# Cross-attention and mixture-of-experts layer: a second load of the next block's rows for in-place normalisation, and H's fp32 copy kept in PSUM

## The reference

```python
x = x + xattn(layernorm(x), ctx_768, ...)
x = x + ffn(layernorm(x), ...)

def xattn(x, y, ...):
    q = (x @ Wq + bq); k = (y @ Wk + bk); v = (y @ Wv + bv)      # 16 heads of 32
    attn = softmax(einsum('bnhd,bmhd->bhnm', q, k) * scale)
    out = einsum('bhnm,bmhd->bnhd', attn, v).reshape(B, N, 512)
    h = relu(out @ W1 + b1)                                      # 1024 wide
    return h @ W2 + b2

def ffn(x, ...):
    top1 = argmax(x @ Wg.T)
    xhat = (x - mu) * rsqrt(var + 1e-5)
    # each token gets its expert's  gelu((xhat * s_e + b_e) @ w1 + b1) @ w2 + b2
```

## Time and profile before

| | us |
|---|---|
| median of three runs (1581.66 to 1583.35) | 1581.79 |
| the profiled execution | 1584.45 |
| its span, first to last instruction | 1582.6 |
| TensorE matmul busy | 1515.4 (96%) |
| VectorE busy | 1037.9 (66%) |
| ScalarE busy | 713.1 (45%) |
| GpSimd busy | 441.9 (28%) |

### The profile page before, as it was taken

How to read it: one execution, slowest core, us unless ns; L and a number is a source line. 1 busy time by engine, 2 the same in 40 slices (tenths; PEclk the granted TensorE clock), 3 DMA queues, 4 the chain that set the end, 5 groups by cost and what they waited for, 6 DMA issues and landing times.

```text
span 1582.6 us, 24339 instructions
## 1 busy us (share of the span) xinstructions
PE 1515.4 (96%) x7988; PEld 1254.6 (79%) x7988; DVE 1037.9 (66%) x2496; ACT 713.1 (45%) x2015; POOL 441.9 (28%) x312
## 2 busy tenths in 40 slices
PE   6799999999999999999999999999999999997998
PEld 3688788787878787878787788878787878776886
DVE  5756566675758576766666675757575757467776
ACT  2545445353535363635444353535353636333443
POOL 3422122121222222212131122122222222136776
PEclk8899999999999999999999999999999999999999
DMA  9200101112020202020101101010101011548773
GB/s 230 80 28 1 54 1 40 42 31 74 3 86 1 74 14 74 22 75 21 61 27 54 34 23 38 17 54 1 54 1 54 1 54 54 215 153 261 232 226 112
DMA packets 67736, 105.93 MB, mean 67 GB/s; under 512 B 26967, under 2 KB 35432, under 8 KB 66591
## 3 DMA queue, kind: packets, MB, share of 16 engines
q1 hardware_dynamic: 56814, 70.68, 15.9%
q0 software_dynamic: 10800, 33.70, 5.5%
HBM read 59.47 MB, written 46.72 MB: 67 GB/s over the span
## 4 chain that ended last, share of the span: by engine, by line
PE 60%; DVE 23%; DMA 7%; ACT 4%; issue 3%; POOL 2%; DVEq 0%; POOLq 0%; SPq 0%; ACTq 0%
PE bank L1025 13%; PE bank L1050 12%; PE bank L887 11%; PE bank L911 5%; PE bank L1005 5%; DMA region<-rows,pos 4%; DVE actH L994 4%; PE bank L1455 4%; PE bank L1499 4%; DMA rows<-in_x 3%; DVE xn L845 2%; POOL region L1193 2%; ACT actH L988 2%; PE bank L1119 2%; PE bank L1438 2%
## 5 line engine op out<-in xcount | busy, mean ns | idle before, releaser
L1050 PE MATMUL bank<-w,actH 128*128 128x512 f32 x1536 | 373.8, 393 | 4.6 <-DVE actH L1040 4.6
L1025 PE MATMUL bank<-actA,w 128*128 128x512 f32 x1536 | 366.7, 394 | 0.0
L1025 PEld LDWEIGHTS bank<-actA,w 128*128 128x128 f32 x1536 | 286.0, 188 | 62.2
L1050 PEld LDWEIGHTS bank<-w,actH 128*128 128x128 f32 x1536 | 282.4, 188 | 62.9 <-DVE actH L1040 8.6
L970 POOL TENSOR_TENSOR E<-E,rc 128x1232 f32<-128x1232 f32 x64 | 145.0, 2265 | 447.6 <-DVE rc L965 447.6
L1040 DVE TENSOR_TENSOR actH<-htmp,actH 128x512 fp32r<-128x512 f32 x128 | 88.7, 693 | 166.8 <-ACT actH L1036 148.1
L1035 ACT ACTIVATE htmp<-bank,b 128x512 f32<-128x512 f32 x128 | 88.2, 689 | 226.1 <-PE bank L1025 217.4
L887 PE MATMUL bank<-actA,wq 128*128 128x512 f32 x768 | 182.0, 390 | 0.0
L943 ACT ACTIVATE E<-bank,mx 128x77 f32<-128x77 f32 x512 | 157.6, 365 | 45.4 <-DVE mx L920 45.4
L887 PEld LDWEIGHTS bank<-actA,wq 128*128 128x128 f32 x768 | 144.2, 188 | 30.4 <-issue 0.5
L1193 POOL DMA_INDIRECT region<-rows,pos x64 | 63.1, 985 | 373.0 <-DVE pos L1187 333.9
(11 more groups left out here) (165 smaller groups left out, 2063.3 us busy)
## 6 DMA issues: line engine op xcount, KB each, us to landing
rowB<-region SPq DMA_DIRECT2D x71, 258.0 KB
rows<-in_x SPq DMA_DIRECT2D x64, 256.0 KB, 3.5
e_raw<-in_E SPq DMA_DIRECT2D x16, 256.0 KB, 2.7
region<-padrow SPq DMA_DIRECT2D x9, 258.0 KB, 2.6
w_raw<-in_W SPq DMA_DIRECT2D x1, 2048.0 KB, 10.3
w_raw<-in_W SPq DMA_DIRECT2D x2, 1024.0 KB, 8.5
e_parts<-e_high SPq DMA_DIRECT2D x8, 256.0 KB, 2.0
e_parts<-e_low SPq DMA_DIRECT2D x8, 256.0 KB, 2.3
```

What stands on the lines that cost most here:

```text
L1025: mm = pe.matmul(p[:], w, a, start=k == 0 and j == 0, stop=k == KD - 1 and j == 2)
L1050: mm = pe.matmul(p[:], a, w, start=m == 0 and j == 0, stop=m == MF - 1 and j == 2)
```

## The change

Three things change, and some steps move.

The rows of the next block are loaded a second time, into four buffers `xn` of their own (step `XNLOAD`, in two halves, after H chunks 0 and 2). The statistics are taken from these, and all four tiles are normalised in place at the end of the chain. The step XSTAT moves from behind chunk 5, where three pieces were given out at once, to behind chunk 4. The rows proper are still loaded behind the scatter.

The addition of b2 to the rows becomes a step of its own, `XB`, on GpSimd. It waits for the landing of the rows and no longer for xn. In the setup the XLOAD of block 0 goes behind VLOAD, and its XB behind XLOAD(1).

ScalarE writes the fp32 value of an H chunk back into the chunk's PSUM bank, behind the high part, and VectorE's subtraction reads it from there. The bank is handed on after that subtraction. `htmp` is gone; E1 and E2 both use the memory of the four xn, and the steps that load and split E2 stand later.

```diff
-    xn = [sb(f"xn{i}", [P, D]) for i in range(2)]
+    xn = [sb(f"xn{i}", [P, D]) for i in range(SUB)]
-    htmp = [sb(f"htmp{i}", [P, BLK]) for i in range(2)]
...
-        step("XLOAD", 0)
+        step("XNLOAD", 0, 0)
+        step("XNLOAD", 0, 2)
         step("XSTAT", 0)
...
         step("VLOAD", 0)
+        step("XLOAD", 0)
...
         step("XLOAD", 1)
+        for s in range(SUB):
+            step("XB", 0, s)
...
+                if not last and m in (0, 2):
+                    step("XNLOAD", b + 1, m)
...
-                if m == MF - 3 and not last:
+                if m == MF - 4 and not last:
                     step("XSTAT", b + 1)
-                    step("DRIP", 3)
...
                 step("YA", b, 0)
-                if prep is not None:
-                    step("E2_RAW", prep)
+                for s in range(SUB):
+                    step("XB", b + 1, s)
                 step("Y", b, 0)
...
-            "H": lambda b, m: (S["act_hh"], MF * b + m + 1),
+            "H": lambda b, m: (S["dve_h"], MF * b + m + 1),
...
+        def sp_xnload(sp, b, s0):
+            for s in (s0, s0 + 1):
+                if b:
+                    sp.wait_ge(S["pe_xT"], SUB * (b - 1) + s + 1)
+                if PREP0 + 2 <= b < PREP0 + 2 + NE:
+                    sp.wait_ge(st_e1 if s0 else st_e2, 32 * (b - PREP0 - 1))
+                sp.dma_start(xn[s][:], A["x"][b * BLK + P * s:b * BLK + P * s + P, :]).then_inc(ld_xn[s], 16)
...
-                    dve.wait_ge(ld_x[b % 2][s], 16 * (b // 2 + 1))
-                    n = issued(dve.bn_stats(bn[:, s, :], rows[b % 2][:, s, 0:D]))
+                    dve.wait_ge(ld_xn[s], 16 * (b + 1))
+                    n = issued(dve.bn_stats(bn[:, s, :], xn[s][:]))
...
-                for s in range(2):
-                    dve_xn(dve, b, s)
+                for s in range(SUB):
+                    dve.tensor_scalar(xn[s][:], xn[s][:], mvx[:, s, 0:1], rx[:, s:s + 1],
+                                      ALU.subtract, ALU.mult).then_inc(S["dve_xn"], 1)
...
-            if s + 2 < SUB:
-                dve_xn(dve, b, s + 2)
-
-        def pool_xT(pool, b, s):
-
-            pool.wait_ge(S["dve_xn"], SUB * b + s + 1)
+
+        def pool_xb(pool, b, s):
+
+            pool.wait_ge(ld_x[b % 2][s], 16 * (b // 2 + 1))
...
-            act.activation(htmp[m % 2][:], of("H", b, m)[:], ACT.Relu, bias=b1[:, m:m + 1]).then_inc(S["act_h"], 1)
-            act.activation(actH[:, 0, m, :], of("H", b, m)[:], ACT.Relu, bias=b1[:, m:m + 1]).then_inc(S["act_hh"], 1)
+
+            act.wait_ge(S["pe_h"], MF * b + m + 1)
+            p = of("H", b, m)
+            act.activation(actH[:, 0, m, :], p[:], ACT.Relu, bias=b1[:, m:m + 1])
+            act.activation(p[:], p[:], ACT.Relu, bias=b1[:, m:m + 1]).then_inc(S["act_h"], 1)
...
-            dve.wait_ge(S["act_hh"], MF * b + m + 1)
-            dve.tensor_tensor(actH[:, 1, m, :], htmp[m % 2][:], f32(actH[:, 0, m, :]), ALU.subtract
+            dve.wait_ge(S["act_h"], MF * b + m + 1)
+            dve.tensor_tensor(actH[:, 1, m, :], of("H", b, m)[:], f32(actH[:, 0, m, :]), ALU.subtract
```

More of the change, by code:

```diff
@@ L108, in xattn_moe_kernel @@
     E, E_at = sb("E", [P, KD, SUB, SC])
-    xn = [sb(f"xn{i}", [P, D]) for i in range(2)]
+    xn = [sb(f"xn{i}", [P, D]) for i in range(SUB)]
     xn_at = xn[0][1]
     xn = [t[0] for t in xn]
-    htmp = [sb(f"htmp{i}", [P, BLK]) for i in range(2)]
-    htmp_at = htmp[0][1]
-    htmp = [t[0] for t in htmp]
     b2bc, _ = sb("b2bc", [P, D])
@@ L213, in xattn_moe_kernel @@
     assert o[0] <= E_at + size([P, KD, SUB, SC], F32)
[L215 to L220, removed]
+    e2_raw = at("e2_raw", [P, D], F32, xn_at)
+    e2_low = at("e2_low", [P, D], F32R, xn_at)
+    e2_high = at("e2_high", [P, D], F32R, xn_at + 4 * D)
+    e1_raw = at("e1_raw", [P, KD, EH], F32, xn_at + 8 * D)
+    e1_acc = at("e1_acc", [P, 2, EH], F32, xn_at + 12 * D)
+    e1_row = at("e1_row", [1, 2, EH], F32, xn_at + 12 * D + 8 * EH)
     o[0] = rows_at[0]
@@ L248, in xattn_moe_kernel @@
             "first", "consts", "wk", "wv", "ctx", "wq", "w1", "w2a", "w2b", "e1", "e2", "eb", "jt", "tab", "pad0", "e1raw", "e2raw")}
+        ld_xn = [sem(f"ld_xn{s}") for s in range(SUB)]
         ld_x = [[sem(f"ld_x{i}_{s}") for s in range(SUB)] for i in range(2)]
@@ L261, in xattn_moe_kernel @@
             "dve_xn pool_xb pe_xT act_xT dve_xT pe_q act_q dve_q pe_s dve_max dve_sub act_es act_exp dve_rc pool_p "
-            "pe_pt act_pt dve_pt pe_av act_o dve_o pe_h act_h act_hh dve_h pe_y dve_x2 dve_row pool_ones pe_gate dve_gate "
+            "pe_pt act_pt dve_pt pe_av act_o dve_o pe_h act_h dve_h pe_y dve_x2 dve_row pool_ones pe_gate dve_gate "
             "pe_tt act_tt dve_tt pe_l act_l pe_lt dve_lg dve_oh pe_rk dve_rk dve_cum dve_pos "
@@ L399, in xattn_moe_kernel @@
                 if prep is not None:
-                    step("E2_HIGH", prep)
[L401 to L409, removed]
+                    step("E2_RAW", prep)
+                    step("E1_RAW", prep)
+                step("Y", b, 1)
+                step("Q", b + 1, 0)
+                step("Q", b + 1, 1)
+                if prep is not None:
+                    step("E2_HIGH", prep)
                 for g, (first, y) in enumerate((("YA", 2), ("Y", 2), ("YA", 3), ("Y", 3))):
@@ L412, in xattn_moe_kernel @@
                         step("S", b + 1, g, s)
+                    if prep is not None and g == 0:
+                        step("E2_LOW", prep)
+                        step("E2_STORE", prep)
                     step("EXP", b + 1, g)
@@ L556, in sp_w2load @@
             sp.dma_start(w2_raw[1][:], A["W2"][:, MF * D // 2:]).then_inc(L["w2b"], 16)
+        def sp_xnload(sp, b, s0):
[5 more added lines that the diff above has]
+                sp.dma_start(xn[s][:], A["x"][b * BLK + P * s:b * BLK + P * s + P, :]).then_inc(ld_xn[s], 16)
+            if b == 0 and s0:
+                sp_setup2(sp)
         def sp_xload(sp, b):
@@ L565, in sp_xload @@
                 sp.dma_start(rows[b % 2][:, s, 0:D], src).then_inc(ld_x[b % 2][s], 16)
-            if b == 0:
-                sp_setup2(sp)
         def sp_kstore(sp):
@@ L619, in sp_e2raw @@
         def sp_e2raw(sp, e):
-            sp.wait_ge(S["dve_h"], MF * (PREP0 + e + 1))
+            sp.wait_ge(S["pe_xT"], SUB * (PREP0 + e + 2))
             sp.dma_start(e2_raw[:], A["E2"][:, e, :]).then_inc(L["e2raw"], 16)
@@ L853, in pe_xT @@
             for k in range(KD):
-                mm = pe.transpose(p[:, P * k:P * k + P], xn[s % 2][:, P * k:P * k + P], ident[:])
+                mm = pe.transpose(p[:, P * k:P * k + P], xn[s][:, P * k:P * k + P], ident[:])
             mm.then_inc(S["pe_xT"], 1)
@@ L1532, in xattn_moe_kernel @@
             "XSTAT": {"dve": dve_xstat},
-            "XT": {"pe": pe_xT, "act": act_xT, "dve": dve_xT, "pool": pool_xT},
+            "XT": {"pe": pe_xT, "act": act_xT, "dve": dve_xT},
+            "XB": {"pool": pool_xb},
+            "XNLOAD": {"sp": sp_xnload},
             "Q": {"pe": pe_q, "act": act_q, "dve": dve_q},
```

6 lines of the change are left out of this document (removed).

## The result

The changed kernel takes 1611.44 us (median of four runs, 1609.87 to 1626.91) where the kernel before takes 1581.72 beside it: a ratio of 1.0209, 95% interval 1.0161 to 1.0256. Its profiled execution took 1610.22, its span is 1608.4. The forecast was 1614, slower. The whole interval lies above 1, so the change is slower; by how much is known less well (1.6 to 2.6%).

What follows compares the result with a forecast made beforehand. TensorE, nearly always busy, was taken as the bound. Held chain +29.1, block 0 +0.3, setup +0.5 and clock +3.3 made +33.2 on the profiled 1584.45; on the median 1615, rounded down to 1614 us; range 1575 to 1634.

Steps and rivals of the forecast that it cites:

- The rival that a run of small steps keeps its turn: VectorE's chain at block ends is held once, by 0.9 us at most: about 1566 to 1578 us; chance 0.15.
- The early load: Second load of rows, issued by SyncE at H steps 0 and 2, lands in time and costs nothing; slack some 5 us.
- The held chain: In 14 block ends, GpSimd's row additions hold VectorE's small steps and normalisations that make xn: +29.1 us; chance 0.74.
- Y-to-Q: Block end, from the start of YA(0) and Y(0) matmuls to Q: 14.62 us before, forecast 16.70.
- my walk: Block-end chain stepped through, each step held until the running addition ends: mean 9.34 us from Y(0)'s start to chunk 7's end.
- The alternation: At block ends, VectorE steps and GpSimd additions take turns: mean 9.34 us; if additions pass waiting steps, 9.52, sum +31.6.
- The undisturbed chain: Block end with nothing held: first transposes 6.2 us after Y(0)'s start, Y-to-Q 13.56, -14.9 us over 14 blocks.
- the fast rival: At block ends the additions do not hold the chain enough: -3 to -15 us in 14 blocks; chance 0.15.
- Clock: Half clock on TensorE after waits before chunk 7, in two of 14 blocks at 1.6 us each: +3.3 us, bounds 0 and 22.
- Setup: Before the blocks: Q 6.4 us earlier, against 5.5 for block 0's additions and 1.5 half clock: +0.5 us.
- Block 0: End of block 0, whose additions run long before its chain: 6.2 + 7.24 against 13.10, +0.3 us.
- PSUM copy: H's fp32 value read by VectorE's subtraction from PSUM instead of SBUF: zero, within 0.3 us a block either way.

Runs made afterwards that it cites:

- (5): Changed kernel with each row addition of blocks 1 to 15 waiting until all four xn tiles are normalised: 1562.25 us, ratio 0.9870 to the kernel before.
- the rows of 9: Changed kernel with each row addition of blocks 1 to 15 done twice: 1677.42 us, ratio 1.0599 to the kernel before.
- Run 1: Changed kernel with each row addition of blocks 1 to 15 waiting also for its own tile's normalisation: 1603.18 us, ratio 1.0121 to the kernel before.
- (6): Changed kernel with block 0's four additions moved behind its last softmax multiplication on GpSimd: 1610.57 us, ratio 1.0185 to the kernel before.
- (3): Kernel before with only the PSUM copy of H's fp32 value added: 1582.93 us, ratio 0.9991 to the kernel before.
- run 2: Changed kernel with chunk 7's low part of H put ahead of the four normalisations, additions still free: 1573.66 us, ratio 0.9943 to the kernel before.
- run 10: Changed kernel with only the third and fourth additions of blocks 1 to 15 waiting for all normalisations: 1575.96 us, ratio 0.9951 to the kernel before.
- the kernel of 4: Changed kernel with chunk 7's low part ahead of the normalisations, additions each behind their own tile's, block 0's behind its last softmax multiplication: 1550.80 us.

## Why the prediction was right, and where its sizes were off

The direction and the mechanism were right. That the number came within 3 us is luck: its largest term was nearly twice too large, and other errors made up for it.

**The mechanism holds as it was told.** The wait for xn in the blocks is gone, one wait for the low part of H stands in its place (39.2 us, forecast 40 to 50; 1.9 to 3.3 each, forecast 2.9 to 3.5), the small steps end with the additions, and without the overlap the change is faster (5). The rival that a run of small steps keeps its turn is refuted: the rows of 9 show one step for one addition, six times over. The early load is early: in block 8 SyncE's queue issued the second pair of xn 8 us ahead of the statistics (793.48).

```profile
785.30 0.81 SPq L568 DMA_DIRECT2D xn<-in_x  x2
```

**The held chain, +29.1 forecast.** The 14 blocks grew by 24.5 us in all; less five half-clock stretches of 1.61, that is +16.4. What was wrong is the size of this term, not its cause. In the nine blocks without half clock Y-to-Q grew from 14.62 to 15.74 (forecast 16.70). The first transposes come there after 8.49, where my walk had 9.34. In block 8 the walk let the additions end 3.8 us after the start of Y(0); they ended after 2.79. They began 2.26 ahead of it instead of 1.84, and took 1.26 each where I had put 1.3 and 0.2 of pause behind each. Statistics and aggregates took 2.91 where I had added up 3.17 from rows that held other work between. The rest, forecast 7.36, is 7.24.

**The alternation.** By the rule of the Trainium skill ("SBUF — State Buffer", Who interferes with whom: issued first holds the ports, the other blocks) my walk gave 9.34, by the row in which an addition seemed to pass a waiting step 9.52. The traces of the blocks agree with the rule: in no row above does a held step wait for a second addition. Why the shift of the earlier trace rows started 0.25 before its addition and yet ended with it stays open.

**The undisturbed chain.** I had 6.2 to the first transposes and 13.56 for Y-to-Q, it is 5.78 and 13.01 (5). So I put the gain of the fast rival too low: without the hold the change gains 22.5 us in 14 blocks, not 14.9. My range's lower end, 1575, would not have held that case; the run with it gave 1562.

**Clock, +3.3 forecast.** It was five stretches of 1.61, +8.1; the price of one was right (1.6), the number was not. I counted only waits of about 3.3 us as long enough, from the two in the earlier trace rows. Run 1 shows that wrong: waits of 1.99 and 1.98, ahead of the same three matmuls, and the one is followed by half clock and the other is not.

```profile
716.76 1.29 PE L1051 MATMUL bank<-w,actH 128*128 128x512 f32 x3 [1.99 <-DVE actH L1041]
...
631.99 0.97 PE L1051 MATMUL bank<-w,actH 128*128 128x512 f32 x3 [1.98 <-DVE actH L1041]
```

What decides between the two is open. Two errors of opposite sign, 12.7 too much for the chain and 4.8 too little for the clock, brought the forecast nearer the time.

**Setup, +0.5 forecast.** It was +1.33. I had the additions cost 5.5 and the half clock behind them 1.5, 7.0 together; H starts 5.5 earlier without them (6). In the rows the four additions keep GpSimd for 4.98, the transposes start at 84.52 instead of 80.43 in 6, 4.1 later, and half clock up to 87.4 costs the other 1.4. The gain of 6.4 that I set against it was 90.15 - 85.94 = 4.2. Here too one error hid the other. GpSimd and TensorE there, in the kernel after:

```profile
77.18 4.98 POOL L879 TENSOR_TENSOR rows<-rows,b2bc 128x512 f32<-128x512 f32 x4
82.13 2.24 POOL L972 TENSOR_TENSOR E<-E,rc 128x1232 f32<-128x1232 f32 x1
```
```profile
84.52 2.86 PE L978 MATMUL bank<-ident,E 128*103 128x128 f32 x12 [4.50 <-POOL E L972]
```

**Block 0,** forecast +0.3 on 13.10, was 13.01. **PSUM copy,** forecast nothing, is nothing (3).

**Sum.** +33.2 forecast on the profiled execution, 25.8 measured between the spans; the medians differ by 29.7. The difference between these two is that the profiled execution of before lay 2.7 above its median and that of after 1.2 below. So 3.9 of the closeness of 1614 to 1611.4 is owed to which executions were profiled.

## What to carry to other kernels

A wait that seems only to delay an engine nobody waits for may be what keeps it off another's way: before removing it, look at what that engine will then run beside. GpSimd's elementwise work belongs beside VectorE's statistics (2.46 us for four with additions beside them or without) or its instructions with an operand in PSUM (0.68), not beside a chain of small steps in SBUF, where each addition of 1.3 us held one step of 0.17 us until it ended. And in a list that one engine walks in order, put the piece that TensorE wants next ahead of the work that only the step after it needs.

## What was not expected

Half clock came after waits as short as 2.0 us (7 of 14 in run 1, all of them 2.0), and none came after waits up to 1.1 us (run 2), up to 1.3 in run 10. Such stretches can make the time of a kernel with regular waits vary: 1609.87 to 1626.91 for the change (mean granted clock 0.983 and 0.974), 1603.45 to 1616.27 in 6, against 1549.09 to 1551.24 for the kernel of 4, in whose blocks TensorE waits for nothing of note.

Statistics and aggregates with one operand in SBUF ran beside the additions at full speed (2.46 for four, 0.38 for four), while the steps and normalisations, which also read only SBUF, were held.
